# An RWKV and FP4 kernel on one Trainium2 core: another order of the stages on all engines

## The reference

```
h = _layernorm(x) * (1 + ca) + sa
x = x + ga * _L0_attn_ref(h, ...)        # two layers of time mix and channel mix
h = _layernorm(x) * (1 + cb) + sb
x = x + gb * _L0_ffn_ref(h, ...)         # silu(fp4(h) @ fp4(gate)) * (fp4(h) @ fp4(up)), then down
# the time mix, per token:
kv = kt[..., :, None] * vt[..., None, :]
out = einsum('bhk,bhkv->bhv', rt, state + u * kv)
state = state * wt[..., None] + kv
```

## Time and profile before

| | |
|---|---|
| median of 3 runs | 2997.3 us (2996.72 to 3000.86) |
| the profiled execution | 2999.92 us, its span 2998.2 us |
| PE | 2764.8 us busy (92%), 32829 matmuls |
| PE's weight loads | 2200.1 us (73%) |
| DVE | 2362.4 us (79%) |
| ACT | 1379.6 us (46%) |
| POOL | 1283.9 us (43%) |
| granted clock of TensorE | 0.978 of full speed on average |

### The profile page before, as it was taken

How to read it: one execution, slowest core, us unless ns; L and a number is a source line. 1 busy time by engine, 2 the same in 40 slices (tenths; PEclk the granted TensorE clock), 3 DMA queues, 4 the chain that set the end, 5 groups by cost and what they waited for, 6 DMA issues and landing times.

```text
span 2998.2 us, 78791 instructions
## 1 busy us (share of the span) xinstructions
PE 2764.8 (92%) x32829; PEld 2200.1 (73%) x32829; DVE 2362.4 (79%) x5345; ACT 1379.6 (46%) x2707; POOL 1283.9 (43%) x1457
## 2 busy tenths in 40 slices
PE   5789999999999999999999999999999999999875
PEld 3567777777777777777777777777777777777653
DVE  5756888888888888878888888888788888878664
ACT  1344444544454455445445545545554444454331
POOL 3344444445444444444444444444444444444320
PEclk7799999999999999999999999999999999999997
DMA  4000000000000000000000000000000000000000
GB/s 149 14 5 9 12 12 5 9 12 12 12 12 12 5 11 10 12 12 12 12 5 12 9 12 13 12 12 9 9 9 12 12 12 12 5 9 12 8 8 7
DMA packets 36831, 41.51 MB, mean 14 GB/s; under 512 B 3272, under 2 KB 35200, under 8 KB 36480
## 3 DMA queue, kind: packets, MB, share of 16 engines
q1 hardware_dynamic: 35696, 36.32, 3.8%
q10 hardware_dynamic: 784, 0.16, 0.1%
HBM read 28.08 MB, written 8.39 MB: 12 GB/s over the span
## 4 chain that ended last, share of the span: by engine, by line
PE 60%; DVE 22%; ACT 8%; issue 6%; POOL 3%; ACTq 0%; DVEq 0%; DMA 0%; POOLq 0%
PE ps_all L1437 10%; PE ps_all L1251 9%; PE ps_all L1259 8%; PE ps_all L1451 6%; PE ps_all L1488 5%; PE ps_all L1470 5%; PE ps_all L1357 4%; DVE sxrk L1120 3%; DVE att L1126 2%; PE ps_all L1243 2%; DVE stats L1018 2%; ACT mixin L906 2%; DVE chan L1064 2%; PE ps_all L1383 2%; PE ps_all L1413 1%
## 5 line engine op out<-in xcount | busy, mean ns | idle before, releaser
L753 POOL TENSOR_TENSOR mixin<-mixin,hT_tm 128x512 f32<-128x512 f32 x320 | 390.3, 1230 | 353.7 <-DVE mixin L1085 353.7
L1437 PE MATMUL ps_all<-chan,cwk 128*128 128x256 f32 x1536 | 375.0, 391 | 8.3 <-DVE chan L1064 5.4
L1120 DVE TENSOR_TENSOR sxrk<-sxrk,dec 128x512 f32<-128x512 f32 x384 | 275.5, 717 | 95.6 <-PE ps_all L1357 92.3
L1451 PE MATMUL ps_all<-cwv,chan 128*128 128x256 f32 x1536 | 343.7, 380 | 0.0
L1437 PEld LDWEIGHTS ps_all<-chan,cwk 128*128 128x128 f32 x1536 | 283.6, 191 | 63.3 <-issue 20.2
L1451 PEld LDWEIGHTS ps_all<-cwv,chan 128*128 128x128 f32 x1536 | 290.3, 191 | 38.7 <-ACT chan L853 0.3
L733 POOL TENSOR_TENSOR rstd<-var,powc 128x2 f32<-128x2 f32 x224 | 188.7, 843 | 239.8 <-DVE var L1024 238.8
L1085 DVE SCALAR_TENSOR_TENSOR mixin<-ps_all,vcol,sxrk 128x256 f32<-128x256 f32 x640 | 270.1, 476 | 21.0 <-PE ps_all L1289 10.7
L1357 PEld LDWEIGHTS ps_all<-sxrk 64*64 64x64 f32 x10240 | 170.1, 130 | 138.3 <-issue 138.2
L772 POOL TENSOR_TENSOR lora<-S,dec 128x256 f32<-128x256 f32 x128 | 91.0, 711 | 355.9 <-DVE S L1135 355.3
L1357 PE MATMUL ps_all<-sxrk 64*64 64x32 f32 x10240 | 202.8, 217 | 43.9 <-DVE att L1126 40.8
(11 more groups left out here) (181 smaller groups left out, 6262.3 us busy)
## 6 DMA issues: line engine op xcount, KB each, us to landing
xin<-in_L_attn_x_dram SPq DMA_DIRECT2D x32, 256.0 KB, 2.7
tok<-in_L_attn_x_dram SPq DMA_DIRECT2D x32, 256.0 KB, 2.7
out_dram<-x SPq DMA_DIRECT2D x32, 256.0 KB, 2.1
cwk<-in_L_attn_cWk_dram SPq DMA_DIRECT2D x2, 768.0 KB, 7.9
cwv<-in_L_attn_cWv_dram SPq DMA_DIRECT2D x2, 768.0 KB, 9.9
ffn_work<-in_L_wmod_dram SPq DMA_DIRECT2D x2, 512.0 KB, 5.3
tok<-in_L_ffn_w_down_dram SPq DMA_DIRECT2D x1, 704.0 KB, 4.3
tok<-in_L_ffn_w_gate_dram SPq DMA_DIRECT2D x1, 640.0 KB, 8.3
```

The source lines that it names most:

```text
L753: pool.tensor_tensor(m, m, hT["tm", l][:, :, :, 1:P + 1].rearrange("p k c t -> p (k c) t"), ALU.add).then_inc(ev["mixed"][b], 1)
L1120: v.tensor_tensor(rko, rko, t, ALU.mult).then_inc(ev["rk_lev"][b], 1)
L1437: ins = pe.matmul(bank(b, "ck", lj, "k")[:, m * TT:(m + 1) * TT], cwk[:, l, k, n:n + P], k_in[:, k, :], start=(k == 0), stop=(k == KC - 1))
L1451: ins = pe.matmul(bank(b, "cv", l, "v")[:, c * D:(c + 1) * D], relu[t // 2][:, t % 2, c * P:(c + 1) * P], cwv[:, l, t, :], start=(t == 0), ...
```

## The change

The tables ORDER, HEAD, TAIL and SECOND have other contents. No instruction is added or taken away, and the loops, buffers and semaphores are the same. The text is one line shorter, so that lines of the kernel after are smaller by one: L1243 has become L1242.

```diff
 ORDER = {
-    PE: """4/4 gu.1.1; 1/2 lev.1; 0/1 yt; 3/3 cr cv; 0/1 wo; 1/2 pv lev.2; 4/4 ht.1; 1/2 lev.3; 2/1 turn.cm; 4/4 dn; 1/2
+    PE: """0/1 ov; 1/2 pr; 4/4 ht.0; 1/2 pw2; 4/4 gu.1.0; 0/1 yt; 4/4 gu.1.1; 1/2 lev.1 pv; 3/3 cr; 1/2 lev.2; 0/1 wo; 3/3
...
-    POOL: """4/5 lna.out; 0/2 mf.0; 1/4 st.0; 0/2 mf.1; 1/4 st.1; 0/2 mf.3; 4/5 lna.ffn; 1/4 gnb; 0/2 mf.2; 1/4 yt; 2/3 cv;
+    POOL: """0/2 st.1; 1/3 mf.2; 0/2 gnb; 1/3 mf.4 tot; 0/2 yt; 2/2 lna.cm; 3/4 cv; 0/1 lna.in; 2/2 cmix; 0/1 lna.tm; 4/5 dn;
...
-SECOND = """0 mf.2 m; 2 turn.cm x; 2 ck.0 k; 2 ck.2 k; 3 turn.cm x; 3 ck.0 k; 3 ck.1 k; 3 ck.2 k; 3 cv v; 4 gu.0.0 g; 4 gu.0.1 g; 4 ht.0
-    b; 4 gu.1.0 u; 4 gu.1.1 u; 4 ht.1 b"""
+SECOND = """0 mf.2 m; 0 so t; 2 ck.1 k; 2 cr r; 2 cv v; 3 turn.cm x; 3 ck.1 k; 3 ck.2 k; 3 cv v; 4 gu.0.0 g; 4 gu.0.1 u; 4 ht.0 a; 4
+    gu.1.0 g; 4 gu.1.1 g; 4 ht.1 b; 4 dn o"""
```

More of the change, by code:

```diff
@@ new lines @@
+    DVE: """4/4 qc.0; 0/1 st.0 st.1 gna gnb; 4/4 gu.1.0; 1/2 mf.4; 4/4 gu.1.1; 1/2 lev.1; 4/4 qa.1; 1/2 lev.2; 0/1 wo; 4/4
+        qc.1; 2/1 lna.cm; 3/3 cv; 1/2 lev.3; 0/0 lna.in; 2/1 lnb.cm; 0/0 lnb.in; 1/2 pg; 0/0 h0 lna.tm; 1/2 lev.4; 0/0
+        lnb.tm; 2/1 cmix; 4/4 dn; 4/3 lna.out; 0/0 mix; 1/2 lev.5; 4/3 lnb.out; 1/2 lev.6; 4/3 x2; 0/0 mf.0; 4/3
+        lna.ffn; 0/0 mf.1; 1/2 st.0; 0/0 mf.3 mf.2; 1/2 st.1 gna; 4/3 lnb.ffn hf; 1/2 gnb; 4/3 qa.x qc.x; 0/0 mf.4; 2/1
+        cv; 1/2 wo; 1/1 lna.tm; 3/2 lna.cm; 0/0 lev.1; 3/2 lnb.cm; 4/3 gu.0.0; 1/1 lnb.tm; 0/0 lev.2; 3/2 cmix; 0/0
+        lev.3; 4/3 gu.0.1; 1/1 mix; 4/3 qa.0; 0/0 pg lev.4; 1/1 mf.0; 0/0 lev.5; 1/1 mf.1 mf.3; 0/0 lev.6; 1/1 mf.2""",
@@ new lines @@
+    AC: """1/4 pk; 4/6 ht.0; 1/4 pr; 4/6 gu.1.0; 1/4 pw2; 4/6 gu.1.1; 0/3 yt; 4/6 qa.1; 3/5 cr; 1/4 pv; 4/6 ht.1; 1/4 pg;
+        2/3 turn.cm; 0/2 turn.tm; 2/3 ck.0 ck.1; 0/2 mix; 1/4 kt; 2/3 ck.2; 1/4 gna; 0/2 pw1 pk pr; 2/3 cr; 4/5 qa.x;
+        1/4 yt; 0/2 pw2; 4/5 xt gu.0.0; 0/2 pv; 3/4 turn.cm; 4/5 gu.0.1; 1/3 turn.tm; 0/2 pg; 3/4 ck.0; 1/3 mix; 4/5
+        qa.0; 3/4 ck.1; 0/2 kt; 3/4 ck.2; 1/3 pw1; 0/2 gna""",
+    POOL: """0/2 st.1; 1/3 mf.2; 0/2 gnb; 1/3 mf.4 tot; 0/2 yt; 2/2 lna.cm; 3/4 cv; 0/1 lna.in; 2/2 cmix; 0/1 lna.tm; 4/5 dn;
+        0/1 mix; 4/4 lna.out; 1/3 st.0; 0/1 mf.0; 4/4 lna.ffn; 0/1 mf.1; 1/3 st.1; 0/1 mf.3; 1/3 gnb; 0/1 mf.2; 1/3 yt;
+        2/2 cv; 0/1 mf.4; 1/2 lna.tm; 3/3 lna.cm; 0/1 tot st.0; 3/3 cmix; 1/2 mix mf.0 mf.1 mf.3""",
@@ L49 @@
 HEAD = {
[L50 to L76, removed]
-        cmix; 1/1 lev.3; 3/0 h0 lna.tm; 1/1 pg; 3/0 lnb.tm; 0/4 lnb.out; 1/1 lev.4; 3/0 mix; 0/4 x2 lna.ffn lnb.ffn; 1/1
-        lev.5; 3/0 mf.0; 1/1 lev.6; 3/0 mf.1 mf.3; 1/1 st.0; 3/0 mf.2; 1/1 st.1 gna gnb; 0/4 hf qa.x qc.x; 2/2 cv; 3/0 mf.4;
-        1/1 wo; 2/1 lna.tm; 3/0 lev.1; 2/1 lnb.tm; 1/3 lna.cm; 0/4 gu.0.0; 3/0 lev.2; 1/3 lnb.cm; 0/4 gu.0.1; 2/1 mix; 0/4
-        qa.0; 1/3 cmix; 3/0 lev.3; 2/1 mf.0 mf.1 mf.3; 3/0 pg lev.4; 0/4 qc.0; 2/1 mf.2; 3/0 lev.5 lev.6; 0/4 gu.1.0; 3/0 st.0
-        st.1 gna; 2/1 mf.4; 3/0 gnb; 0/4 gu.1.1 qa.1; 2/1 lev.1; 0/4 qc.1; 1/3 cv; 3/0 wo; 3/2 lna.cm; 2/1 lev.2; 3/2 lnb.cm;
-        4/0 lna.in lnb.in""",
```

243 lines of the change are left out of this document (137 added, 106 removed).

## The result

The changed kernel takes **3040.0 us** (median of 4 runs, 3036.0 to 3040.5), the kernel before in the same session 2997.0 (2996.2 to 3000.9). The ratio is 1.0135, with a 95% interval from 1.0123 to 1.0147: slower by 43 us. The forecast was 3019, slower by 22, and 3040.0 lies within its range of 2960 to 3045.

The account below looks back on a forecast made before the run. PE (TensorE) was taken as the bound, so only its idle time could move. Added waits of 3.2 us per block against 2.4 removed gave 22 us more over 27 blocks, fill and drain at nothing: 3019 us, range 2960 to 3045.

Parts of the forecast that it names:

- Removed: Five PE waits in the steady part, 64.3 us or 2.4 us per block, claimed to go under the new order.
- E: Small PE waits: mf.0 of stream 0 0.2; pw1 and wo of stream 0 and turn of stream 2 together 0.2.
- I take all 64.3 us off: Step that counted all five steady PE waits as removed in full, as the best case for the change.
- A: Mix of stream 0 on PE waits for DVE's lerp, which needs POOL's shift: 1.2 us per block, ends 0.8 and 1.6.
- B: lev.2 of stream 0 and turn of stream 3 on PE wait for DVE: 0.8 us per block, ends 0.3 and 1.3.
- C: ck.0 of stream 3 on PE waits for the bank of gu.0.1's gateT product: 0.3 us per block, ends 0 and 0.8.
- D: lev.5 of stream 0 on PE, with only four mf products between lev.4 and it: 0.5 us per block.
- I price both at nothing, from 8 less to 8 more: Fill and drain, the start and end of the run: no net change in us, an estimate.
- The prediction's own test: If steady PE waits are as listed but the total is not 3019, the fill or the drain has moved.
- The rival on POOL: POOL held at mix of stream 0 by DVE products, twice 0.68 per block: 37 us more, 3056 us; chance 0.06.
- the rule: Trainium skill: DVE instructions with two SBUF inputs and GpSimd instructions reading SBUF lock each other out for the whole instruction.

Follow-up runs that it names:

- b1_tanh: Kernel before with lev.4 of stream 0 moved on PE between mix and mf.0 of stream 1, steady list only: 2997.2 us.
- b2_lev3: Kernel before with pg of stream 1 ahead of lev.3 on PE, and pv and pg ahead of turn.cm on ACT, steady list only: 2993.8 us.
- s3_small_add: Changed kernel with POOL's shift of stream 0 ahead of the add of dn, and that add cut from 512 to 16 elements per partition: 3023.3 us.
- experiment 5: Changed kernel with POOL's shift of stream 0 ahead of the add of dn, 3051.3 us; the same with that add cut short, 3023.3 us.
- two mixed kernels: Order of before up to the third dn, then that of the change: 3028.1 us; the mirror image: 3017.1 us.
- experiment 2: Changed kernel with the set-up stages (streams 5 and 6) put back behind the same stages as in before, in the fill list: 3050.7 us.
- three single swaps: Kernel before, separately: lev.4 of stream 0 moved, 2997.2 us; pg of stream 1 ahead of lev.3, 2993.8; pk of stream 0 ahead of so, 3049.6.

## Why the prediction was right in direction and half the size

- **Removed, 2.4 us per block.** Right at all five places: lev.3, the tanh, so and pw1 of stream 1 and lev.1 of stream 0 wait no more in one block's timeline. The 9.7 us of pw1 and the 6.2 of the tanh in the new list are stream 0's, and belong to E. What now covers lev.3, wo and cv, comes from ahead of lev.2; pv and cr stood there in both orders, other than the section on the change says. But the step "I take all 64.3 us off" rests on waits being independent. They are not: b1_tanh only moved one, b2_lev3 took its own off in full.
- **A, 1.2.** Too high. The wait on PE is 13.6 over 26, 0.52; by s3_small_add the place costs at most 0.67 per block. Both are under my lower end of 0.8. PE's own work came out right: 14.3 us from lev.3 (1498.28) to mix (1513.12) without the wait of 0.52, where I had 14.2. The chain was sized too long: 14.5 us from the start of DVE's cv (1498.46) to the end of the lerp, where I had 15.4. Two of its rows in before held the lock of experiment 5. The shift took 1.29 there and 1.04 here. And my run "without a break" of 9.00 us had a wait of 0.20 in it and an h0 of 1.65 us beside a shift of POOL, where h0 takes 0.87 in the changed kernel (from 1503.35). In before:

```profile
1565.55 1.65 DVE L1047 SCALAR_TENSOR_TENSOR xin<-mixin,rstd,rows 128x256 f32<-128x256 f32 x2 [0.20 <-POOL rstd L733]
```

```profile
1565.49 1.04 POOL L738 TENSOR_TENSOR chan<-hT_cm 128x512 f32<-128x512 f32 x1
```

- **B, 0.8.** lev.2 0.78 and turn 0.29, 1.07 in all, inside the ends, and at the two stages that I named.
- **C, 0.3.** No wait of its own is listed. The sign that I gave for it, ck.0 waiting for a bank, did not show.
- **D, 0.5.** lev.5 waits 0.42. Right.
- **E, 0.4.** The tanh of stream 0 is 0.21 (0.2 forecast), pw1 of stream 0 0.41 (0.2 forecast, with two others).
- **Not forecast:** lev.6 of stream 0 0.33 and ov 0.46 and 0.15. The first has a visible source. DVE's half of lev.5 takes 1.65 us in the changed kernel beside POOL's add of mf.0 of stream 1, which began 0.08 earlier:

```profile
1555.70 1.65 DVE L1119 TENSOR_TENSOR sxrk<-sxrk,dec 128x512 f32<-128x512 f32 x1 [0.16 <-PE ps_all L1356]
```

```profile
1555.62 1.18 POOL L752 TENSOR_TENSOR mixin<-mixin,hT_tm 128x512 f32<-128x512 f32 x1 [6.30 <-DVE mixin L1084]
```

The group over the whole run, in the page of before and in that of the changed kernel:

```profile
L1120 DVE TENSOR_TENSOR sxrk<-sxrk,dec 128x512 f32<-128x512 f32 x384 | 275.5, 717 | 95.6 <-PE ps_all L1357 92.3
```

```profile
L1119 DVE TENSOR_TENSOR sxrk<-sxrk,dec 128x512 f32<-128x512 f32 x384 | 316.0, 823 | 44.9 <-PE ps_all L1356 33.6
```

The same 384 instructions took 40.5 us longer, in the one place of DVE that stands between two levels. DVE's total fell all the same, from 2362.4 to 2350.3. Other instructions got shorter: those of L586 (now L585) in the rounding to FP4 took 109.0 us in before and 82.6 in the changed kernel, and the added shift (L1047, now L1046) is the h0 shown under A. That the longer products are why lev.6 and ov wait is argued from the timeline; no run took the overlap away there.

In sum the waits of one block are 3.57 us, 3.3 in the mean, where I had 3.2, and the steady part lost 0.86 per block (87.99 less 87.13) where I had 0.8. That it comes so close is in part luck: A is 0.5 to 0.7 too high and C 0.3, and three waits of 0.94 in all had no term. The 22 us forecast for it came out as 18.3 over 22 blocks. **The step that failed is "I price both at nothing, from 8 less to 8 more"**: the fill cost 16 us by the dn starts (12 and 17 in the two mixed kernels), the drain 5, 21 together and beyond my 8. Which places of the fill lose it stays open, as said in experiment 2. The prediction's own test for this holds: the waits are as listed within a few tenths, and the total was not 3019. I had argued that most of the idle time in the first 100 us is a serial chain that both orders walk. But the loss comes behind it. The product of wo in block 0 is even 2.9 us earlier (83.04 for 85.93), and block 1's is 5.8 later (169.37 for 163.59).

**The rival on POOL.** I said that both of POOL's rows speak against the rule. I misread one: the shift of 1.29 us was held for 0.25 by DVE's product, as experiment 5 shows. The add of 1.27 only shows that no DVE instruction with two SBUF inputs had started ahead of it. The 37 us that the rival put on A did not come, since in the changed kernel neither of POOL's two operations there was held (1.27 and 1.04). The lock does act in this kernel, also on DVE, and in the steady part of the forecast it had no term.

## What to carry to other kernels

Beside the waits of the busiest engine, read through which engines the chain that ended last runs, before and after a change of order: PE was 92% busy in both kernels, but its part of the chain fell from 60% to 20%. A listed wait need not be worth its length: of three single swaps one gave the whole wait in the steady part, one nothing, and one took nearly five times as much, so each is to be tried alone. When a duration from a timeline goes into a sum, compare it with the same instruction elsewhere in the trace: two that I used were 0.25 and 0.8 us too long. A steady order and its fill list are one thing: price the fill apart, and when editing the steady list look from which block each engine's edit takes hold, since 14 us lay in that, of which 10 came back when the seam was mended.

## What the hardware showed that I had not expected

A DVE instruction with two SBUF inputs stood still for most of the time that POOL's tensor_tensor ran beside it: the lerp of 0.88 us took 1.87 beside an add of 1.27 (0.22 us of add: no delay), and a product of 0.69 took 1.65 beside one of 1.18. DVE's mixes that take one operand from PSUM did not slow: four of them from 1557.60 took 1.65 us, 0.41 each as elsewhere, though POOL's next two adds began at 1558.55 in their midst. Nor does every operation of POOL do it. The power for the root, on two elements per partition, ran for 0.70 us beside the lerp of 0.88 in the changed kernel and did not hold it. The held instruction shows no wait in the profile: it starts on time and is longer.
